# The causal triangle of the score blocks: one matmul of 128 rows per head in place of two of 64 rows

## The reference, cut to what matters

```python
q, k, v = jnp.split(qkv, 3, axis=-1)          # 16 heads of 8
scores = jnp.einsum('bhqd,bhkd->bhqk', q, k) * (1.0 / np.sqrt(HD))
causal = (jnp.arange(t)[:, None] >= jnp.arange(t)[None, :]).astype(scores.dtype)
scores = scores * causal - (1.0 - causal) * NEG
attn = jax.nn.softmax(scores, axis=-1)
out = jnp.einsum('bhqk,bhkd->bhqd', attn, v)
```

## Time and profile before

| what | us |
|---|---|
| runs, median (lowest to highest of 3) | 1457.5 (1452.84 to 1466.6) |
| the profiled execution | 1454.24 |
| its span, first to last instruction | 1452.4 |
| causal attention, first fill to last scores | 99.4 to 479.3 |

### The profile page before, as it was taken

How to read it: one execution, slowest core, us unless ns; L and a number is a source line. 1 busy time by engine, 2 the same in 40 slices (tenths; PEclk the granted TensorE clock), 3 DMA queues, 4 the chain that set the end, 5 groups by cost and what they waited for, 6 DMA issues and landing times.

```text
span 1452.4 us, 29994 instructions
## 1 busy us (share of the span) xinstructions
PE 1361.0 (94%) x11934; PEld 492.8 (34%) x11996; DVE 1165.7 (80%) x1356; ACT 1050.2 (72%) x2053; POOL 148.4 (10%) x430
## 2 busy tenths in 40 slices
PE   8986999999999999889879999999999999999989
PEld 4242333332333363434413333333233323333633
DVE  6676898999997065655699999999999999993454
ACT  3544778888889824423449999999999999999121
POOL 9103321211111000000000000000000000000000
PEclk9988999999999999989869999999999999999799
DMA  4045000000000000000312000000000000000000
GB/s 99 1 113 136 16 5 7 11 5 4 12 4 3 5 9 1 0 0 1 113 41 68 26 4 12 4 4 3 12 4 4 4 4 11 4 4 5 9 0 30
DMA packets 31740, 28.80 MB, mean 20 GB/s; under 512 B 11728, under 2 KB 28208, under 8 KB 31600
## 3 DMA queue, kind: packets, MB, share of 16 engines
q1 hardware_dynamic: 31600, 26.88, 6.9%
HBM read 17.03 MB, written 9.70 MB: 18 GB/s over the span
## 4 chain that ended last, share of the span: by engine, by line
DVE 50%; PE 41%; ACT 3%; SPq 3%; issue 2%; DMA 1%; POOL 0%; DVEq 0%; POOLq 0%; ACTq 0%
DVE m_blockmax L1205 46%; PE ps L1112 8%; PE ps L1057 5%; PE ps L1093 4%; PE ps L576 3%; PE ps L587 3%; PE ps L577 3%; SPq L1275 3%; PE ps L247 2%; PE ps L328 2%; ACT m_prob L1190 2%; PE ps L234 1%; PE ps L350 1%; PE ps L240 1%; PE ps L1144 1%
## 5 line engine op out<-in xcount | busy, mean ns | idle before, releaser
L1205 DVE TENSOR_REDUCE m_blockmax<-ps 128x2 f32<-128x1024 f32 (+2 forms) x832 | 911.5, 1156 | 46.1 <-PE ps L1057 33.4
L1190 ACT ACTIVATE m_prob<-ps 128x512 f32<-128x512 f32 (+3 forms) x1664 | 849.1, 575 | 70.5 <-PE ps L1093 56.4
L1112 PE MATMUL ps<-m_prob,m_v_op 128*16 128x256 f32 (+1 forms) x6400 | 513.7, 381 | 9.7 <-ACT m_pv L1173 8.8
L1057 PE MATMUL ps<-m_k_all,m_q_all 64*128 64x512 bf16 (+3 forms) x1664 | 320.7, 383 | 27.4 <-DVE m_blockmax L1205 24.9
L1093 PE MATMUL ps<-m_q_max,m_k_all 64*128 64x512 bf16 (+3 forms) x1664 | 331.8, 367 | 0.0
L1057 PEld LDWEIGHTS ps<-m_k_all,m_q_all 64*128 64x128 bf16 x1664 | 79.9, 93 | 356.0 <-DVE m_blockmax L1205 187.8
L1112 PEld LDWEIGHTS ps<-m_prob,m_v_op 128*16 128x16 f32 x6400 | 108.5, 94 | 225.2 <-issue 161.8
L1093 PEld LDWEIGHTS ps<-m_q_max,m_k_all 64*128 64x128 bf16 x1664 | 139.6, 94 | 99.5 <-ACT m_prob L1190 56.8
L1229 POOL CAST m_maxparts<-m_negmax 128x8 bf16<-128x8 f32 x64 | 14.1, 220 | 1001.8 <-DVE m_negmax L1213 990.3
L663 ACT ACTIVATE m_prob<-ps 128x512 f32<-128x512 f32 x40 | 23.3, 593 | 72.7 <-PE ps L576 72.7
L1181 ACT ACTIVATE m_q_max<-ps 128x512 bf16<-128x512 f32 x64 | 38.3, 598 | 41.7 <-PE ps L1079 41.1
(11 more groups left out here) (207 smaller groups left out, 981.2 us busy)
## 6 DMA issues: line engine op xcount, KB each, us to landing
ba_parts<-m_part SPq DMA_DIRECT2D x8, 384.0 KB, 3.4
ea_parts<-m_part SPq DMA_DIRECT2D x8, 384.0 KB, 2.9
m_k_all<-ea_parts SPq DMA_DIRECT2D x84, 32.0 KB
m_q_all<-ea_parts SPq DMA_DIRECT2D x84, 32.0 KB
m_k_all<-ba_parts SPq DMA_DIRECT2D x36, 64.0 KB
m_q_all<-ba_parts SPq DMA_DIRECT2D x36, 64.0 KB
ba_sums<-m_pv SPq DMA_DIRECT2D x128, 9.0 KB
ea_sums<-m_pv SPq DMA_DIRECT2D x128, 9.0 KB
```

The source lines that it names most:

```text
L1057: mm = pe.matmul(ps[:, MX + 2 * (u % 2) + j, 0:width], q_all[head, pair, q0:q0 + TW], k_all[head, pair, CW * kc:CW * kc + width], start=Tr ...
L1112: mm = pe.matmul(ps[VC * g:VC * g + VW, SUM, a + o:b + o], v_op[:, i, 2 * pair + j, :], prob[:, (2 * t + j) % NP, a:b], start=(i == 0), st ...
L1190: nc.scalar.activation(prob[:, (2 * t + j) % NP, q0:CW], ps[:, e % ST, q0:CW], ACT.Exp, scale=SCALE)\
L1205: nc.vector.tensor_reduce(blockmax[:, m % plan.AHEAD, qt, :, kc], ps[:, MX + 2 * (u % 2):MX + 2 * (u % 2) + 2, 0:width], AX.X, ALU.max)\
```

## The change

The triangle is added by one matmul of all 128 rows for each head, with `identb` as weights and `mask_q` as the moving operand, in place of two of 64 rows for each head. The two tensors of halves, the eight copies, and SyncE's wait ahead of them go, and `LATE_IN` counts eight copies fewer.

```diff
--- before.py
+++ after.py
@@ -103,8 +103,6 @@
         k["select"] = n.sb("select", [P, 2, 3, 2, P], bf16)
         k["max_ones"] = n.sb("max_ones", [P, 1], fp32)
         k["mask_q"] = n.sb("mask_q", [P, TW], bf16)
-        k["ident_h"] = n.sb("ident_h", [P, 2, TW], bf16)
-        k["hide_q"] = n.sb("hide_q", [P, 2, TW], bf16)
         k["pick"] = n.sb("pick", [3 * EXPERTS, EXPERTS // 2, 2, ED], bf16)
         k["spread"] = n.sb("spread", [P, SUB, HEADS, HD], fp32)
         k["maxparts"] = n.sb("maxparts", [P, TPC, P], bf16)
@@ -134,14 +132,8 @@
         for name in ("e_gate", "e_up"):
             sp.dma_start(k[name][:, :, :], dram[name].rearrange("e h d -> h e d")).then_inc(self.late_in, 16)
         sp.dma_start(k["e_down"][:, :, :], dram["e_down"].rearrange("(g e) d h -> (e d) g h", e=2)).then_inc(self.late_in, 16)
-        sp.wait_ge(self.made, self.TWIST_MADE)
-        for half, whole in (("ident_h", "identb"), ("hide_q", "mask_q")):
-            for j in range(2):
-                for h in range(2):
-                    sp.dma_start(k[half][HALF * j:HALF * j + HALF, h, :], k[whole][HALF * h:HALF * h + HALF, :])\
-                        .then_inc(self.late_in, 16)
-
-    EARLY_IN, LORA_IN, LATE_IN = 16 * len(EARLY), 16 * len(LORA), 16 * (len(LATE) + 3 + 8)
+
+    EARLY_IN, LORA_IN, LATE_IN = 16 * len(EARLY), 16 * len(LORA), 16 * (len(LATE) + 3)
 
     def dve(self, dve):
         nc, k = self.nc, self.k
@@ -1057,11 +1049,9 @@
                 mm = pe.matmul(ps[:, MX + 2 * (u % 2) + j, 0:width], q_all[head, pair, q0:q0 + TW],
                                k_all[head, pair, CW * kc:CW * kc + width], start=True, stop=True)
             if causal and kc == c:
-                for h in range(2):
-                    for j in range(2):
-                        head = slice(HALF * j, HALF * j + HALF)
-                        mm = pe.matmul(ps[:, MX + 2 * (u % 2) + j, width - TW:width], k["ident_h"][head, h, :],
-                                       k["hide_q"][head, h, :], start=False, stop=True, skip_group_check=True)
+                for j in range(2):
+                    mm = pe.matmul(ps[:, MX + 2 * (u % 2) + j, width - TW:width], k["identb"][:, :],
+                                   k["mask_q"][:, :], start=False, stop=True, skip_group_check=True)
             mm.then_inc(self.mx_filled, 1)
 
         def turn_max(m):
```

## The result

The changed kernel runs at 1.0078 of the time before, 95% interval 1.0054 to 1.0102: 11.4 us more on 1457.5, where 11 were forecast. The plain medians, over 21 runs of each, are 1475.09 and 1458.59 us, 16.5 us apart; the ratio leaves out the three runs of the changed kernel that lie over 1.5% above its fastest. The runs spread widely (1460.76 to 1490.2 against 1452.84 to 1471.7). So the time alone places the effect only between 7.9 and 14.9 us, and the traces have to say what it is made of.

What follows compares the result with a forecast made beforehand. The prediction took TensorE to bound most of the causal attention after 141 us, behind SyncE's loads. Passes and loads 0, changes of tile shape 11 us, start 0: 1457.5 + 11 = 1468.5 us (+0.75%), range 1459 to 1479.

Steps and rivals of the forecast that it cites:

- What bounds it: Causal attention: SyncE's loads of q and k decide until 141 us, then TensorE time added to the loop mostly reaches the end.
- 0.10 us each way for a change of tile shape: At each triangle with scores behind it, into full height and back: two changes, 0.20 us added.
- Loads hidden: Triangle's weight loads, four becoming two: hidden before and after the edit, so counted as nothing.
- 58 with scores behind them, 36 covered: Last 95 triangles: 58 before scores cost 0.20 us each, 11.6 us; 36 before a fill cost nothing, hidden by VectorE waits.
- the floor from the chain: Causal attention: triangles on the old chain of waits, with the added changes, give at least 10.1 us.
- other 13: Triangles with scores behind them where the chain is on VectorE: some come through, so 11 us was taken between 10.1 and 11.6.
- The start: SyncE's queue: eight copies and a wait go, 5 us less in front of 56 us of idle time, worth nothing.
- nothing moves before 141 us: Stretch before the sums come back: hidden by SyncE's queue, so the 33 triangles there cost 0.
- VectorE takes it: Rival for the loop: only the stretch after 300 us counts, 24 triangles, 4.8 us, 1462 us; chance 0.12.
- Everything comes through: Rival for the loop: VectorE's waits give no cover, all 95 triangles count, 19 us, 1476.5 us; chance 0.15.
- Loads (23 us): Rival at the triangle: each full-height matmul waits out its load, 0.40 us on the 58, 1480.5 us; chance 0.03.
- Not slower: Rival at the triangle: height changes freely, cost stays 0.11 us, up to 5.8 us come off, 1451.7 to 1457.5; chance 0.08.

Runs made afterwards that it cites:

- e2: The kernel before with only the triangle's matmuls made full height, the two tensors, eight copies and wait left in; 1.0089 of before, loop 374.1 us.
- e6: The kernel before with full-height triangles only in chunk 0 (32 of 128), half-height elsewhere; 1.0035 of before, loop 363.8 us.
- e7: The kernel before with full-height triangles only in chunks 1 to 3 (96 triangles), half-height in chunk 0; 1.0062 of before, loop 374.3 us.
- e3: The changed kernel with the full-height triangle put ahead of the fill's own matmuls; 1.0022 of before, loop 368.0 us.
- e1: The changed kernel run again with no edit; 1.0097 of before, loop 373.0 us.
- e5: The kernel before profiled again with no edit, a single run without a ratio; loop 362.5 us, sums sent at 146.8 us.
- e8: The changed kernel with one half-height pass per triangle, each row standing for two queries; 0.9951 of before, loop 361.5 us.

## Why the prediction was right, point by point

- **What bounds it.** TensorE in the loop after SyncE's wait. Shown by e2, e6 and e7: in the loop the 96 late triangles cost 10 us and the 32 early ones, beside SyncE's queue, nothing.
- **Two passes stay two passes.** Right: 0.11 us before and after.
- **0.10 us each way for a change of tile shape.** Right to the rows' last digit: 0.10 in and 0.11 back at 322.98 and 323.20, none towards a turn. e3 is the test of it: one change taken away, half the loss gone (from 363.2 to 358.1, with 353.3 before), with the passes unchanged.
- **Loads hidden.** Right for the second of the two full-height loads. The rule in the Trainium skill, TensorE: Matmul & The Clock Gate, Part 3 ("The mechanism"), would by the estimate of the prediction have put 0.40 on a triangle; 0.20 was measured. The prediction doesn't say that the load behind a change of shape isn't pulled ahead; it has the price of the change without what it is made of. The Trainium skill says that a change of tiling mode drains TensorE, and gives no price (TensorEngine Tiling (Array Packing), Key Properties: "Mode switching requires drain"). This trace has 0.10 us at each change of shape, and can't tell a drain from a load in the open.
- **58 with scores behind them, 36 covered.** One of the 58, at 132.1 us, lies before the sums come back, so the loop has 57. At like clock (before against changed and e1) the loop grew by 10.3 us, and behind its first 40 sums by 10 in the changed kernel, e1, e2 and e7. That is the floor from the chain, 10.1, and not TensorE's 11.6: of the "other 13" of which some were to come through, next to nothing arrived. The 11.4 and 11.6 in the loops of e2 and e7 are not that upper end but half clock at the start. TensorE's waits fell by 5.0 us, so the cover was used and not used up, though some of the 36 never had any.
- **The start.** The copies and the wait were worth nothing that can be measured, and the shifted layout too: e2.
- **The total.** 11 forecast, 11.4 by the ratio, 10.3 by the loop. That the ratio lands on 11 is in part luck: its interval is 7.9 to 14.9 us, and the same triangles gave 14.1 and 13.0 in e1 and e2.
- **Where I said I would be wrong.** "if the loop's end moves by under 8 or over 14 us": it moved by 21.7 in the profile, and time did change before 141 us, which I had ruled out. The step that failed is the statement that nothing moves before 141 us. A profile of one execution can't test it: two profiles of the kernel before have the first sums sent 13.2 us apart (133.6 and 146.8 us). Whether the edit itself moves anything there on the average stays open (e5, e6). The sign should have been the loop's length, which grew by 10.3. One profile of each kernel would have put the loss at 20.9 us, twice what the loop gives.
- **The rivals.** VectorE takes it: no, +10.3 and not +4.8. Everything comes through (19 us): no. Loads (23 us): no. Not slower: no.

## What to carry to other kernels

On TensorE count passes and changes of tile shape, not instructions: here two half-height matmuls beside each other were one pass, and full-height ones between half-height neighbours cost 0.20 us more than they stream. If they are needed, put them next to others of the same tile shape, or where a change of shape is paid anyhow; in this kernel the order alone gave back half of the loss. The price of an addition can be bounded from below by walking the old chain of waits; the same walk is only an upper bound for what a removal gives, and here with a second engine close by it gave about half.

## What the runs showed that I had not expected

The same twelve of SyncE's copies (64 KB each) took 6.20 and 9.97 us of its queue in two executions of the same kernel, and TensorE's first sums after its wait started at 141.2 and 157.1 us. That is 15.9 us of spread between two executions of one program, more than the effect under study. The stretch behind the loop, which no edit touches, took between 944 and 953 us in the ten profiles. And a difference of 1 us in the loop came from the length of half clock at its start: 3 us in both profiles of the kernel before and in both of the changed one, 6 in e2, e6, e7 and e8. What sets it these rows don't say. A difference of single profiles is to be split by stretches before it is read.
